# A query scratch laid out by head, its loads moved ahead of the last sums, and maxima turned in another PSUM bank

## The chip, the cores and the metric

One Trainium2 chip, one of its cores. The metric is the device time of one execution in microseconds; of several executions the median counts. The engines are named TensorE (PE in the rows, PEld its weight loads), VectorE (DVE), ScalarE (ACT), GpSimd (POOL) and SyncE (SP); SyncE issues most of the transfers, one after the other.

## What is computed

A block of three sublayers on 4 x 256 tokens of width 512: half a mixture-of-experts step, attention, half a mixture-of-experts step with the same weights. Only the attention matters here:

```python
NUM_HEADS = 32; HEAD_DIM = 16
qkv = hidden_states @ Wqkv
q = qkv[..., :512].reshape(B, S, 32, 16)
k = qkv[..., 512:528]; v = qkv[..., 528:]          # one key and value head for all
scores = einsum('bqhd,bkd->bhqk', q, k) * scale
scores = where(causal, scores + slopes * (pos_k - pos_q), -1e30)
probs = softmax(scores, axis=-1)
attn = einsum('bhqk,bkd->bqhd', probs, v).reshape(B, S, 512)
return attn @ Wo
```

The input is float32, and the scores are formed with float32's accuracy: a query or key value is split into three bfloat16 parts, and a score is the sum of six products of parts.

## The kernel before

The program is written engine by engine. Each engine runs its list in order, and semaphores are the only ties between them. There are four batches (b) of 256 tokens with 32 heads; a group (q, 0 to 7 in a batch) is four heads; n = 8 b + q counts groups over all batches.

**Projections.** In five items per batch (four quarters of the queries, and keys with values) TensorE multiplies, ScalarE takes the first bfloat16 part out of PSUM (L817 for queries, L811 for keys), VectorE forms the rest (L1253), GpSimd the two lower parts (L596, L598). SyncE stores the three parts to DRAM (`q_dram`, L384, and `k_dram`, L382), and loads them back turned, so that the contraction rows of the score products lie on partitions: 96 rows (16 dimensions times six products of parts), for queries in `qside`, for keys in `kT`. ScalarE may write a quarter's first part again only when the store of the batch before has landed.

`qside` has two halves in turn, one for even and one for odd batches, and each batch is loaded in two halves of 16 heads by `q_rows` (L386; its six loads are L394). For batches 2 and 3 this takes place while batches 0 and 1 are attended. Such a load waits for `st_done`, the last use of the rows it overwrites.

**Scores and maxima.** For batch b + 1, `scores` (L1686 to L1688) forms a head's scores with queries on partitions, in two banks in turn, and VectorE reduces each to row maxima (L1264). A product may not start before the maximum of the head two places ahead is taken. Of 16 heads the maxima are joined (L1270), turned by TensorE (`max_turn`, L1721), negated by ScalarE (L839), split by GpSimd (`maxima_parts`, L614 to L617), stored (L407) and loaded as three more rows of `qside` (L410, `m_rows`). In the same groups `scores_t` (L1700, L1702) forms the scores of batch b transposed, with the maxima's rows in the product, ScalarE takes the exponential (L861), GpSimd zeroes the later tokens (L647), and `weigh` (L1714) multiplies by the values into bank `PS_O`. The even groups' results are copied to `aT` (L827), the odd ones' to `odd` (L831). `scores_t` of group 4 needs the second half's maxima of its own batch (`m_in1`).

**Sums.** The values carry columns of ones, so each group's result also holds the sums of the exponentials. SyncE moves them into `sums`: those of an even group by `sums_of_even` (L436), those of an odd one by `odd_in` (L444), which then moves the rest of `odd` into `aT` (L446). When all four pairs of a batch are in, VectorE inverts them in two halves (L1287; L1277 for batch 2), ScalarE and GpSimd split the inverse into parts (L846, L653 to L658), TensorE spreads them over the partitions (`inverse_rows`, L1731), VectorE normalises (L1300), and TensorE multiplies by Wo (`out_part`, L1738). The bank `PS_A` serves `inverse_rows`, `out_part` and, but for the first half of batch 0, `max_turn`. So `max_turn` waits there for the normalisation (q = 4) or for the residual sum (q = 0).

SyncE's order at the end of a batch is: sums of pair 3, odd sums of pair 3, query loads of batch b + 2 (heads 16 to 31), maxima's rows of batch b + 1 (second half). TensorE's order in a group is written out by hand in the loop that begins at L1777.

## Time and profile before

| | us |
|---|---|
| median of 3 runs | 447.17 |
| lowest, highest | 444.88, 447.20 |
| the profiled execution | 446.26 |
| its span, first to last instruction | 444.2 |

Durations in the rows come from the one profiled execution. Times in them are microseconds from the start of its span, so that 2.1 us of its 446.26 lie outside. In the span the first feed-forward stage ends at about 137 us, the projections at about 193 us, the attention at about 313 us; the rest is the second feed-forward stage. The mean granted TensorE clock is 0.985 of full speed.

A timeline row gives the start, the duration, the engine, the line, what is written and read, the number of instructions merged into the row and, in brackets, the idle time of the engine ahead of it with what ended it. A row of SPq is SyncE issuing a transfer, not the transfer. In the chain of waits each piece is the start, the length and what it was.

### The profile page before, as it was taken

The numbers are of one execution on the slowest core, as the hardware profiler recorded it, in microseconds if no ns is written. First come the engines' busy times: TensorE is split into PE (matmuls) and PEld (weight loads), VectorE is DVE, ScalarE is ACT, GpSimd is POOL, SyncE is SP. The second block draws the span as 40 slices with busy tenths as digits, with TensorE's granted clock in tenths as the row PEclk, the third lists the DMA queues.
The fourth block names the chain that finished last, engine by engine and source line by source line (L and its number), as shares of the span: only waits on it lengthen the run. The fifth ranks groups of instructions, "written<-read, shape, count | busy, mean of one in ns | idle before, by whom it ended". The sixth has DMA issues, their size and how long they took to land.

```text
span 444.2 us, 8306 instructions
## 1 busy us (share of the span) xinstructions
PE 394.1 (89%) x2788; PEld 276.5 (62%) x2789; DVE 258.3 (58%) x638; ACT 177.3 (40%) x302; POOL 176.5 (40%) x268
## 2 busy tenths in 40 slices
PE   0799899999969998989979989889999879999972
PEld 0677578888646766555555555344687558888660
DVE  4579643332457975687775685466539933333357
ACT  1321246656202222157654464653340336665300
POOL 2431226666302772355544354452001055666300
PEclk9999999999998999999999999989999999999997
DMA  7999994544289468323133030010420043534278
GB/s 234 291 379 303 316 338 139 176 116 144 111 296 294 131 170 175 96 83 93 29 96 93 8 95 19 10 38 27 155 96 1 0 142 116 161 122 150 90 290 324
DMA packets 51052, 66.05 MB, mean 149 GB/s; under 512 B 8190, under 2 KB 30374, under 8 KB 50980
## 3 DMA queue, kind: packets, MB, share of 16 engines
q1 hardware_dynamic: 42652, 43.55, 31.1%
q0 software_dynamic: 6368, 19.32, 13.9%
q10 hardware_dynamic: 2000, 2.76, 2.0%
q8 instruction: 18, 0.29, 0.3%
q14 instruction: 14, 0.11, 0.1%
HBM read 46.32 MB, written 19.79 MB: 149 GB/s over the span
## 4 chain that ended last, share of the span: by engine, by line
PE 59%; DVE 16%; DMA 12%; SPq 6%; issue 4%; ACT 1%; POOL 1%; ACTq 0%; DVEq 0%; POOLq 0%
PE ps L1588 15%; PE ps L1595 7%; PE ps L1452 6%; PE ps L1738 6%; PE ps L1573 4%; SPq L394 4%; PE ps L1714 3%; PE ps L1657 3%; DMA turns<-in_L_ffn_sw_dram 3%; DMA q_dram<-arena 3%; PE ps L1686 3%; PE ps L1493 2%; DMA arena<-xn_dram,arena 2%; DVE arena L1264 2%; PE ps L1688 2%
## 5 line engine op out<-in xcount | busy, mean ns | idle before, releaser
L1264 DVE TENSOR_REDUCE arena<-ps 128x3 f32<-128x384 f32 x128 | 69.4, 555 | 33.7 <-PE ps L1688 31.6
L1588 PE MATMUL ps<-arena,wj 128*128 128x128 f32 x608 | 74.1, 274 | 0.0
L1588 PEld LDWEIGHTS ps<-arena,wj 128*128 128x128 f32 x608 | 71.0, 192 | 1.0 <-issue 1.0
L861 ACT ACTIVATE arena<-ps 128x768 f32<-128x768 f32 x64 | 51.2, 810 | 43.1 <-PE ps L1702 42.1
L647 POOL TENSOR_SCALAR_AFFINE_SELECT arena<-arena 128x512 f32<-128x512 f32 x64 | 40.7, 641 | 56.7 <-ACT arena L861 56.2
L1159 DVE SCALAR_TENSOR_TENSOR arena<-ps,arena 128x128 f32<-128x128 f32 x38 | 13.3, 351 | 80.1 <-ACT arena L753 80.1
L1452 PE MATMUL ps<-arena,turns 128*128 128x256 f32 x256 | 57.6, 381 | 0.6 <-DMA turns<-in_L_ffn_sw_dram 0.6
L1452 PEld LDWEIGHTS ps<-arena,turns 128*128 128x128 f32 x256 | 48.1, 190 | 9.0 <-issue 2.1
L553 POOL DMA_INDIRECT arena<-xn_dram,arena x34 | 33.2, 978 | 50.8 <-DVE arena L1099 25.2
L558 POOL DMA_INDIRECT y_dram<-arena x38 | 38.4, 1011 | 33.8 <-DVE arena L1166 25.5
L1686 PE MATMUL ps<-cb 128*128 128x256 bf16 x128 | 35.3, 276 | 5.2 <-DVE arena L1264 4.0
L1595 PE MATMUL ps<-w,arena 128*128 x76 | 39.1, 596 | 0.6 <-DVE arena L1159 0.6
L758 ACT COPY wj<-w 128x1024 f32 x38 | 39.6, 1047 | 0.0
L1493 PE MATMUL ps<-turns,arena 128*128 128x512 f32 x64 | 31.9, 623 | 3.6 <-issue 3.6
L749 ACT COPY arena<-ps 128x512 f32<-128x512 f32 x38 | 22.3, 587 | 30.9 <-PE ps L1573 30.9
L1688 PE MATMUL ps<-arena 116*128 116x256 bf16 x128 | 34.6, 270 | 0.0
L1657 PE MATMUL ps<-arena,wj 128*128 128x256 f32 x128 | 31.6, 383 | 1.4 <-ACT arena L801 1.4
L707 ACT ACTIVATE arena<-ps,shb 128x256 f32<-128x256 f32 x16 | 7.6, 473 | 57.9 <-PE ps L1452 57.9
L1738 PE MATMUL ps<-turns,arena 128*128 128x512 f32 x64 | 30.0, 604 | 0.0
L1714 PE MATMUL ps<-arena 128*32 128x128 f32 (+1 forms) x512 | 28.1, 338 | 1.4 <-POOL arena L647 1.4
L1573 PEld LDWEIGHTS ps<-cf,arena 128*128 128x128 f32 x136 | 16.6, 140 | 19.6 <-issue 17.7
L1687 PE MATMUL ps<-arena 116*128 116x128 bf16 x128 | 28.2, 220 | 0.0
(196 smaller groups left out, 586.3 us busy)
## 6 DMA issues: line engine op xcount, KB each, us to landing
arena<-y_dram SPq DMA_DIRECT2D x16, 512.0 KB, 7.4
arena<-q_dram SPq DMA_DIRECT2D x36, 128.0 KB, 2.7
xn_dram<-arena SPq DMA_DIRECT2D x16, 256.0 KB, 5.3
w<-in_L_ffn_ew_dram SPq DMA_DIRECT2D x4, 1024.0 KB, 11.0
q_dram<-arena SPq DMA_DIRECT2D x16, 192.0 KB, 2.4
x<-_attn_hidden_states_dram SPq DMA_DIRECT2D x4, 512.0 KB, 6.2
out_dram<-x SPq DMA_DIRECT2D x8, 256.0 KB, 5.9
arena<-arena SPq DMA_DIRECT2D x30, 64.0 KB
```

What stands on the lines that cost most here:

```text
L647: pool.affine_select(diagonal, diagonal, [[0, 2], [0, 2], [1, P]], ALU.is_ge, 0.0, base=0, channel_multiplier=-1).then_inc(sem("sel"), 1)
L861: act.activation(pr[:, n % 2, pair, :], ps[:, bank:bank + 2, :].rearrange("p a b -> p (a b)")[:, 0:768], ACT.Exp).then_inc(sem("exp"), 1)
L1264: dve.tensor_reduce(m3[:, h // (HEADS // 2), :, h % (HEADS // 2)], ps[:, bank, 0:3 * P].rearrange("p (n k) -> p n k", n=3), AX_X, ALU.max) ...
L1452: ins = pe.matmul(o, sw12[:, c, cols], xnT[:, 2 * pair:2 * pair + 2, c, :], start=(c == 0), stop=(c == KC - 1))
L1493: ins = pe.matmul(ps[:, z_bank(t), :], hidden[t // 2 % 2][:, c, t % 2 * P:(t % 2 + 1) * P], sw3s[:, c, :], start=(c == 0), stop=(c == SHAR ...
L1588: ins = pe.matmul(o, wj[:, par, c, n * INTER:(n + 1) * INTER], xgT[:, par, c, :], start=(c == 0), stop=(c == KC - 1))
L1595: pe.matmul(ps[:, PS_Y + par, :], hj[:, par, :], w3[:, ds(e, 1), :], start=True, stop=True).then_inc(sem(f"y{f}"), 1)
L1657: ins = pe.matmul(ps[:, PS_ST + c, 0:SEQ], wq[:, k, c * P:(c + 1) * P], xaT[b % 2][:, k, :], start=(k == 0), stop=(k == KC - 1))
L1686: pe.matmul(o.rearrange("p (n k) -> p n k", k=P)[:, 0:3:2, :], identb, mask, start=True, stop=True)
L1688: pe.matmul(o[:, P:3 * P], qside[0:R_MAX, p, h, P:2 * P], kT[0:R_MAX, b, :], start=False, stop=True, skip_group_check=True).then_inc(sem(" ...
L1714: ins = pe.matmul(o, vv[:, b, k, 1 - n % 2:1 - n % 2 + 2 * HD], pr_blocks(n % 2, h // 2)[:, k * QT:(k + 1) * QT - k, h % 2, :], start=(k = ...
L1738: ins = pe.matmul(ps[:, at_bank(b, t), :], aT[b % 2][:, c, t * P:(t + 1) * P], wo[:, c, :], start=(c == 0), stop=(c == KC - 1))
```

## The change

It does four things.

- `q_dram` is laid out by batch, head, dimension, part, where it was batch, part, head and dimension. The 96 rows of a product are ordered anew: 48 rows are the three query parts against the first key part, 48 are the query parts 0, 0, 1 against the key parts 1, 2, 1. It is the same six products.
- `q_rows` loads its half with four transfers, one of 48 rows and three of 16, where it had six of 16. The keys are stored by three transfers still, the first of them reading its part three times.
- At the end of a batch, the query loads stand ahead of the odd sums of the last pair.
- `max_turn` writes to the upper half of bank `PS_O`, whose lower half takes the weighed values (but for the first half of batch 0). It is called inside `weigh`, ahead of the weighing, and the next weighing waits until ScalarE has copied the turned maxima. The waits that kept `PS_A` free for it are dropped.

```diff
-QPART = (0, 0, 0, 1, 1, 2)
-KPART = (0, 1, 2, 0, 1, 0)
+QPART = (0, 0, 1)
-        q_dram = nc.dram_tensor("q_dram", (BATCH, 3, DIM, SEQ), BF16).ap()
-        k_dram = nc.dram_tensor("k_dram", (BATCH, HD, len(KPART), SEQ), BF16).ap()
+        q_dram = nc.dram_tensor("q_dram", (BATCH, HEADS, HD, 3, SEQ), BF16).ap()
+        k_dram = nc.dram_tensor("k_dram", (BATCH, 2, HD, 3, SEQ), BF16).ap()
...
-        def m_bank(b, half):
-            return PS_S if (b, half) == (0, 0) else PS_A
+        def turned(b, half):
+            return ps[0:HEADS, PS_S, 0:P] if (b, half) == (0, 0) else ps[0:HEADS, PS_O, SEQ:SEQ + P]
...
-                        for at, count in K_RUNS:
-                            sp.dma_start(k_dram[b, :, at:at + count], kp[:, 0:count]).then_inc(sem("k_out"), 16)
+                        sp.dma_start(k_dram[b, 0], kp[:, 0:1].to_broadcast([HD, 3, SEQ])).then_inc(sem("k_out"), 16)
+                        sp.dma_start(k_dram[b, 1, :, 0:2], kp[:, 1:3]).then_inc(sem("k_out"), 16)
+                        sp.dma_start(k_dram[b, 1, :, 2], kp[:, 1]).then_inc(sem("k_out"), 16)
                     else:
-                        sp.dma_start(q_dram[b, :, c * P:(c + 1) * P, :].rearrange("k p t -> p k t"), qp[:, :, c, :]).then_inc(sem(f"q_out{c}"), 16)
+                        sp.dma_start(q_dram[b, c * 8:(c + 1) * 8].rearrange("h d k t -> (h d) k t"), qp[:, :, c, :]).then_inc(sem(f"q_out{c}"), 16)
...
-                for r in range(len(QPART)):
-                    sp.dma_start(qside[r:R_REST:SPREAD, p, first:last],
-                                 q_dram[b, QPART[r], first * HD:last * HD].rearrange("(h d) t -> d h t", d=HD)
+                sp.dma_start(qside[0:3 * HD, p, first:last], q_dram[b, first:last].rearrange("h d k t -> (d k) h t")
+                             ).then_inc(sem(f"q_in{p}{0 if first == 0 else 1}"), 16)
+                for r in range(3):
+                    sp.dma_start(qside[3 * HD + r:R_REST:3, p, first:last],
+                                 q_dram[b, first:last, :, QPART[r]].rearrange("h d t -> d h t")
                                  ).then_inc(sem(f"q_in{p}{0 if first == 0 else 1}"), 16)
...
                 sums_of_even(4 * b + 3)
-                odd_in(4 * b + 3)
                 if b + 2 < BATCH:
                     q_rows(b + 2, HEADS // 2, HEADS)
+                odd_in(4 * b + 3)
...
+            behind = [0]
+
-            def weigh(n):
+            def weigh(n, turn=None):
 
                 b = n // 8
-                pe.wait_ge(sem("sel"), 2 * n + 2)
                 if n >= 1:
                     pe.wait_ge(sem("oT"), n)
+                if turn is not None:
+                    pe.wait_ge(sem("m_copy"), 2 * turn[0] + turn[1])
+                    max_turn(*turn)
+                    behind[0] = 2 * turn[0] + turn[1] + 1
+                elif behind[0]:
+                    pe.wait_ge(sem("m_copy"), behind[0])
+                    behind[0] = 0
+                pe.wait_ge(sem("sel"), 2 * n + 2)
...
             def inverse_rows(b, half):
 
                 pe.wait_ge(sem("inverse"), b + 1)
-                pe.wait_ge(sem("m_copy"), min(2 * b + 4 + half, 2 * BATCH))
-                if half == 1:
+                if b >= 1:
+                    pe.wait_ge(sem("att_x"), QT * b)
+                if half == 1 and inverse_bank(b, 1) == PS_A:
                     pe.wait_ge(sem("normed"), 2 * b + 1)
...
                     if n >= 1:
-                        weigh(n - 1)
-                    if q == 0:
-                        if b >= 2:
-                            pe.wait_ge(sem("att_x"), QT * (b - 1))
-                        max_turn(b, 1)
-                    if q == 4 and more:
-                        if b == 0:
-                            pe.wait_ge(sem("m_copy"), 2)
-                        else:
-                            pe.wait_ge(sem("normed"), 2 * b - 1)
-                        max_turn(b + 1, 0)
+                        weigh(n - 1, (b, 1) if q == 0 else (b + 1, 0) if q == 4 and more else None)
+                    elif n == 0:
+                        pe.wait_ge(sem("m_copy"), 1)
+                        max_turn(0, 1)
+                        behind[0] = 2
```

SyncE's list at the end of batch 0 (the same at the end of batch 1), before: the even and odd sums of pair 3, the six query loads (L394), the store and the two loads of the maxima's rows.

```order
L436 DMA arena<-arena 4x256 [waits oT]
L444 DMA arena<-arena 4x256 [waits oT]
L446 DMA arena<-arena 64x256 [waits even_sums1]
L394 DMA arena<-q_dram 16x16x256 [waits st_done,q_out3,q_out2]
L394 DMA arena<-q_dram 16x16x256 x5
L407 DMA m_dram<-arena 32x3x128 [waits m_parts]
L410 DMA arena<-m_dram 3x16x128 [waits m_out]
```

The same place in the changed kernel, whose lines lie four further on (L440, L448 and L450 are the sums, L395 and L398 the query loads, L411 and L414 the maxima's rows):

```order
L440 DMA arena<-arena 4x256 [waits oT]
L395 DMA arena<-q_dram 48x16x256 [waits st_done,q_out3,q_out2]
L398 DMA arena<-q_dram 16x16x256 x3
L448 DMA arena<-arena 4x256 [waits oT]
L450 DMA arena<-arena 64x256 [waits even_sums1]
L411 DMA m_dram<-arena 32x3x128 [waits m_parts]
L414 DMA arena<-m_dram 3x16x128 [waits m_out]
```

Four query loads now stand between the even and the odd sums, and the maxima's store follows the odd sums directly.

TensorE's list at the end of the fifth group (q = 4) of batch 1, before: the weighing (L1714), the turned maxima (L1721), scores of the next group, and further down the second half of the spread inverse (L1731).

```order
L1714 MATMUL ps<-arena 32x256 [waits oT,sel]
L1714 MATMUL ps<-arena 32x256 x3
L1714 MATMUL ps<-arena 32x128 x4
L1721 MATMUL ps<-cf,arena 32x128 [waits m_nm,normed]
L1686 MATMUL ps<-cb 128x2x128 [waits s_max]
...
L1731 MATMUL ps<-arena,cb 128x256 [waits normed,m_copy,inverse]
```

The same place in the changed kernel (L1734 turns the maxima, L1727 weighs, L1745 spreads the inverse):

```order
L1734 MATMUL ps<-cf,arena 32x128 [waits m_nm,m_copy,oT]
L1727 MATMUL ps<-arena 32x256 [waits sel]
L1727 MATMUL ps<-arena 32x256 x3
L1727 MATMUL ps<-arena 32x128 x4
L1690 MATMUL ps<-cb 128x2x128 [waits s_max]
...
L1745 MATMUL ps<-arena,cb 128x256 [waits normed,inverse]
```

The turned maxima moved ahead of the weighing, and the wait for the normalisation went from them.

## Rows read from the trace of the kernel before

**Rows 1.** The page's part 1: busy us (share of span) and instructions of each engine.
```profile
PE 394.1 (89%) x2788; PEld 276.5 (62%) x2789; DVE 258.3 (58%) x638; ACT 177.3 (40%) x302; POOL 176.5 (40%) x268
```

**Rows 2.** Timeline of SyncE in the projections: start, us, line, transfer.
```profile
149.27 1.25 SPq L382 DMA_DIRECT2D k_dram<-arena  x3
...
158.93 3.82 SPq L394 DMA_DIRECT2D arena<-q_dram  x6
162.79 3.81 SPq L382 DMA_DIRECT2D k_dram<-arena  x3
```

**Rows 3.** The chain of waits in the projections: start, us, what.
```profile
167.12 2.31 DMA q_dram<-arena
...
174.20 6.05 DMA q_dram<-arena
```

**Rows 4.** Timelines of ScalarE and TensorE in the projections, idle time in brackets.
```profile
168.78 0.37 ACT L811 ACTIVATE arena<-ps 16x256 bf16<-16x256 f32 x1 [4.45 <-DMA k_dram<-arena]
...
180.33 0.88 ACT L817 CAST arena<-ps 128x256 bf16<-128x256 f32 x2 [4.45 <-DMA q_dram<-arena]
...
170.45 0.28 PE L1686 MATMUL ps<-cb 128*128 128x256 bf16 x1 [0.96 <-DVE arena L1264]
...
181.76 0.28 PE L1686 MATMUL ps<-cb 128*128 128x256 bf16 x1 [0.98 <-DVE arena L1264]
```

**Rows 5.** Windows: stretch, engines' busy us, TensorE clock, DMA share, GB/s.
```profile
166.00:167.00 1.00, 1.00 (x7) 0.46 (x6) 0.44 (x1) 0.00 (x0) 0.34 (x1) 1.00 0.59 129
...
175.00:176.00 1.00, 0.25 (x3) 0.07 (x1) 0.86 (x3) 0.58 (x1) 0.46 (x2) 1.00 1.21 185
```

**Rows 6.** Timeline of SyncE at the end of batch 0.
```profile
220.16 0.50 SPq L446 DMA_DIRECT2D arena<-arena  x1
220.77 5.06 SPq L394 DMA_DIRECT2D arena<-q_dram  x6
225.88 0.61 SPq L407 DMA_DIRECT2D m_dram<-arena  x1
```

**Rows 7.** Timeline of TensorE, end of batch 0 and fifth group of batch 1.
```profile
217.82 0.27 PE L1702 MATMUL ps<-arena 119*128 119x256 bf16 x1
...
228.35 0.27 PE L1688 MATMUL ps<-arena 116*128 116x256 bf16 x1
230.48 0.38 PE L1700 MATMUL ps<-arena 119*128 119x512 bf16 x1 [1.85 <-DMA arena<-m_dram]
...
234.03 0.28 PE L1721 MATMUL ps<-cf,arena 128*32 128x128 f32 x1 [0.46 <-DVE arena L1300]
```

**Rows 8.** Timelines of VectorE and SyncE where reciprocals start, batches 0 and 2.
```profile
222.09 0.95 DVE L1287 RECIPROCAL arena<-arena 128x128 f32<-128x128 f32 x1
...
224.69 3.36 DVE L1264 TENSOR_REDUCE arena<-ps 128x3 f32<-128x384 f32 x6
...
285.87 0.50 SPq L446 DMA_DIRECT2D arena<-arena  x1
...
287.77 1.75 DVE L1277 RECIPROCAL arena<-arena 128x256 f32<-128x256 f32 x1 [2.71 <-DMA arena<-arena]
```

**Rows 9.** Timelines of GpSimd and TensorE, the inverse of batch 0.
```profile
228.74 0.66 POOL L658 TENSOR_TENSOR arena<-arena 128x256 bf16<-128x256 f32 x1
...
231.08 0.82 PE L1731 MATMUL ps<-arena,cb 128*128 128x256 bf16 x6
```

**Rows 10.** Timelines of GpSimd and TensorE, the same place of batch 2.
```profile
262.56 0.66 POOL L658 TENSOR_TENSOR arena<-arena 128x256 bf16<-128x256 f32 x1
...
263.37 0.38 PE L1700 MATMUL ps<-arena 119*128 119x512 bf16 x1 [0.89 <-DMA arena<-m_dram]
...
263.98 0.82 PE L1731 MATMUL ps<-arena,cb 128*128 128x256 bf16 x6
```

**Rows 11.** The loads of L394: issue ns min/median/max, first and last start.
```profile
L394 SPq DMA_DIRECT2D arena<-q_dram x42: 560/609/1769, 151.1 to 258.0; - x42
```

**Rows 12.** Window in batch 3, columns as in rows 5.
```profile
292.00:294.00 2.00, 2.00 (x13) 0.84 (x15) 1.15 (x2) 0.69 (x1) 0.00 (x0) 0.50 0.10 33
```

## What the change will do: the prediction

> **What bounds the kernel now.** I read the page's busy shares first, then the chain that ended last through the attention stage (140 to 312 us), then the idle time of TensorE in that stage with its releasers, and last SyncE's issue times, because all edits but one sit on that queue. TensorE is busy 89% of the span [rows 1]; the two feed-forward stages touch nothing of the change, so its price is the sum of the waits of TensorE that it shortens or makes. Three places count.
>
> *The projections, 155 to 181 us.* The chain runs over SyncE: a block of six query loads takes 3.82 us to issue, three key stores behind it 3.81 us (elsewhere the same three took 1.25), then a query store lands, then the next block of loads, then a store issued at 174.20 that lands 6.05 us later [rows 2, 3]. ScalarE waits 4.45 us for the key stores and again 4.45 us for that store; TensorE loses only 0.96 and 0.98 us to the two, 1.94 in all [rows 4]. While the second block drains, the DMA engines are full and move 185 GB/s [rows 5].
>
> *The fifth group of batch 1, 228 to 231 us.* TensorE stands 1.85 us for the maxima's rows [rows 7]. They are late since their store is issued at 225.88, behind six query loads (5.06 us) that are themselves behind the odd sums' two copies, the second issued at 220.16 [rows 6]. The same group of batch 2 stands 0.89 us [rows 10].
>
> *The normalisation's wait.* At 234.03 TensorE waits 0.46 us for VectorE before it turns the maxima, as both use one PSUM bank [rows 7]. This stands twice, in batches 1 and 2.
>
> **The change, part by part.**
>
> *Four loads for six.* Same bytes, same 512 B pieces. One load takes 0.609 us (median of 42, 0.56 at least) [rows 11], with the gap behind it 0.65; each block of six becomes 2.6 us for 3.9, so 1.3 us less. The new first load has three times the rows of the others. No row shows a load of that form; the 256 KB loads among the 42 have twice the rows of the 128 KB ones, and the median and minimum hold for both, so I take 0.65 for it too. In the projections the block at 158.93 ends 1.3 us earlier, so key stores, the store at 167.12, the next block and the landing at 180.25 follow 1.3 earlier, if nothing else holds them. Bounds: 0, if the 3.81 us of the key stores is the queue waiting for the loads to drain (then they end when they did); 1.94, all that TensorE loses there, if those stores also fall towards their 1.25. The second block's faster issue gives nothing: its 1.5 MB drain at the DMA engines' rate and the store lands behind them. I take **-1.3**.
>
> *The layout.* Query stores become 384 rows of 512 B in place of 128 times three, the first key store 48 rows in place of 16. They are as many bytes over the same queue; I take 0, with the two bounds just given as its bounds too.
>
> *The loads ahead of the last odd sums.* SyncE may start when the last transposed scores of batch 0 are done, 217.82 + 0.27 = 218.1 [rows 7]. Four loads end at 220.7; the two copies follow at 220.7 and 221.3, and the maxima's store at 221.85 in place of 225.88. Its rows land about 4 us earlier, TensorE needs them only 2.0 us earlier (the product began at 230.48; the one ahead of it at 228.35, so it stood ready at about 228.45), so that wait goes.
>
> But a wait takes its place. The second copy is issued at 221.3 in place of 220.16, 1.1 us later. VectorE's reciprocal started at 222.09, 1.93 us after that copy's issue; at 285.87 and 287.77, with nothing in the queue and VectorE plainly waiting, the distance is 1.90 [rows 6, 8]. So the reciprocal hangs on this copy already, without slack, and behind it VectorE is booked to 228, its last six maxima without a gap [rows 8]. Call its delay D. It is 1.1 at least. With 786 kB of loads ahead in the queue the copy lands no sooner than 218.1 + 1.9 + their transfer: at 185 GB/s (4.25 us) 224.25, D = 2.2; at 202 GB/s, which the loads reach with no backlog (131 kB in 0.65 us), 3.9 us and D = 1.8. Below 3.2 us of transfer D is 1.1. The short block lies nearer to the free-running case, which issue alone limits, so I take 1.5.
>
> In the projections' trace the store issued behind 1.5 MB of loads took 6.05 us, so small transfers do wait their turn [rows 3]. The Trainium skill (DMA: Bandwidth & Descriptors, Queues, rings and completion order) says the same: on each DMA engine the descriptors of one issuing queue are consumed in ring order. By that rule alone the moved loads would always cost the sums their whole transfer; by the latency alone they cost the 1.1 us of issue.
>
> VectorE's delay passes whole to TensorE, whose scores wait for each maximum. So the wait of 2.03 us gives 2.03 - D. Then another wait stands up: the low part of the inverse, from GpSimd, was ready at 228.74 + 0.66 = 229.40, hangs on the same reciprocal and moves by D too; the product that spreads it stood at 231.08 and can now start at 229.5 + D [rows 9]. Gain there 1.58 - D. For batch 2 the product stood at 263.98 and the inverse was ready at 263.22 [rows 10]: 0.66 - D, that is, a loss.
>
> *Turning the maxima in the other bank.* It removes the two 0.46 us waits. TensorE goes on to scores whose maxima are done; the next consumer, the second half of the spreading, wants that same normalisation, which ended just before 234.03, and TensorE gets there a group's half later, about 234.5. So 0.46 each, nothing late behind. The new order puts one transposition ahead of the weighing and makes the next weighing wait for ScalarE's copy; that copy comes directly behind ScalarE's output copy, a whole group ahead of the next weighing, so 0. In batch 3, where the sums' path sets the end, the transposition counts once: its row lists 0.28 us, of which pipelining hides the most, so +0.1 [rows 7]. The dropped waits for the last maxima copy were long met: 0.
>
> **Sum.** Batch 1: 1.58 + 0.46 - D = 2.04 - 1.5 = 0.54 gained. Batch 2: 0.66 + 0.46 - 1.5 = 0.38 lost. Projections 1.3 gained, batch 3 0.1 lost: -1.3 - 0.54 + 0.38 + 0.1 = **-1.4 us**. Against the profiled execution that is 442.8 us of span, 444.9 of 446.3 in time; that execution lies 0.9 us below the median, so on the median 447.2 - 1.4 = **445.8 us**.
>
> **Rivals.**
>
> *All of it comes:* the key stores fall back, D = 1.1. -1.94 - 0.94 - 0.02 + 0.1 = -2.8, 444.4 us. For: three stores at 1.25 us show that 3.81 is not their own cost. Against: it needs both, and the stall at 163 may stand elsewhere again (a load at 222 took 1.77 us with no visible reason, the maximum in rows 11).
>
> *The issue time is no bound:* nothing in the projections, D about 1.8. -0.24 + 0.68 + 0.1 = +0.5, 447.7 us. For: the longest piece of that chain, 6.05 us, is a landing behind a full queue [rows 3]. Against: SyncE issues without a gap from 158.93 to 166.65.
>
> *The sums drown behind the loads (slower).* Place: the last odd copy of batches 0 and 1. If four larger loads are fed faster than the engines take them, at 302 GB/s against 202 before, and they drain as slowly as the row at 166 us (129 GB/s with the engines only 0.59 busy) [rows 5], say 142, the transfer is 5.5 us and D = 3.5: 1.46 + 2.38 + 0.1 - 1.3 = +2.6, 449.8 us. Moved loads lose as soon as D passes 2.2 in both batches, even with the projections' gain; by over 0.5% from 3.3. Against: 185 GB/s is the rate at the deepest queue the trace has.
>
> *The clock.* At 292 to 294 us TensorE ran 2.00 us at a granted 0.50, 1.2 GHz, behind waits of over 1 us [rows 12]. Those waits stay, but if the fall comes at another moment, what ran in this row takes half: 1.0 us less, 444.8; or as much more, should one fall come at the new waits.
>
> **How the numbers follow.** A measurement of this kernel tells about 0.5% (2.2 us) from no change. Forecast 0.42, all of it 0.26, no bound at issue 0.14, drowned sums 0.12, clock helping on top of the forecast (443 to 445) 0.06. Faster by over 0.5%: 0.26 + 0.06 = 0.32; slower: 0.12; within: 0.56. The forecast's own range runs from D = 1.1 (445.0) to no gain in the projections and D = 2.2 (-(-0.16) + 1.08 + 0.1 = +1.3, 448.5). The range reaches down to the full gain with the clock's 1.0 (443.3) and up to 448.8, short of the drowned case.
>
> **What would show it.** Blocks of loads at 2.6 us; key stores of batch 1 under 2.5 us or still 3.8; ScalarE's second 4.45 us wait about as long, but ended near 179. TensorE's 1.85 and 0.89 us waits for the maxima's rows gone, VectorE's first reciprocal 1.1 to 2.2 us behind its last maximum, released by a transfer, and short TensorE waits for maxima and for the inverse behind it. No wait on the normalisation ahead of the turned maxima. I am wrong if the reciprocal's delay is over 2.2, if the wait for the maxima's rows stays, or if the first large load takes well over 0.65 us to issue.

## The result and the profile after

The changed kernel takes **449.27 us** (median of 17 executions, 446.54 to 455.52), the kernel before, run beside it on the same chip, 446.03 (17, 443.41 to 449.73). The ratio is 1.0075, 95% interval 1.0048 to 1.0103: some 3 us slower. The forecast was 445.8 with a range up to 448.8, so it was wrong, and in sign. Ratios here and below leave disturbed executions out, the medians do not, so that the two can differ (most where the loads alone were moved, six of ten left out).

The profiled execution has a span of 448.7 us against 444.2. I cut both at three events on TensorE: the first projection product, the first main score, and the transposition of the fourth token tile in the second feed-forward, which waits for VectorE in both:

| stretch | before | after | difference |
|---|---|---|---|
| up to the projections | 137.83 | 136.39 | -1.44 |
| projections | 55.71 | 60.01 | **+4.30** |
| main attention | 118.83 | 118.02 | -0.81 |
| second feed-forward | 131.83 | 134.28 | +2.45 |

The first and last rows hold no edit. In the twelve whole kernels of this study the last row lies between 131.7 and 135.1 us with the same code in it, so its 2.45 is nothing that the change can be blamed for on one execution. The projections are where the change lost; the forecast had -1.3 there.

The projections as one window, before and after (columns as in [rows 5]: the first is the length, the next TensorE's busy time, the last three clock, DMA share and GB/s):

```profile
137.83:193.54 55.71, 50.84 (x291) 36.73 (x289) 41.24 (x91) 13.52 (x33) 28.36 (x50) 1.00 0.61 147
...
136.39:196.40 60.01, 52.48 (x290) 37.18 (x289) 41.24 (x91) 13.41 (x33) 28.38 (x50) 0.97 0.65 133
```

Of the 4.30 us, 2.66 are idle time of TensorE (7.53 against 4.87) and 1.64 are the same products taking longer at a lower clock. Over the whole span TensorE's busy time grew by 5.8 us (399.9 against 394.1).

SyncE's timeline in the projections (start, us, line, transfer), beside [rows 2]. L395 is the 48-row load, L398 the three 16-row loads, L382 to L384 the key stores, L328 the load of the turned keys, L386 query stores:

```profile
157.93 0.32 SPq L395 DMA_DIRECT2D arena<-q_dram  x1
158.30 1.94 SPq L398 DMA_DIRECT2D arena<-q_dram  x3
160.28 0.61 SPq L382 DMA_DIRECT2D k_dram<-arena  x1
160.93 0.58 SPq L383 DMA_DIRECT2D k_dram<-arena  x1
161.56 0.83 SPq L384 DMA_DIRECT2D k_dram<-arena  x1
162.43 3.26 SPq L386 DMA_DIRECT2D q_dram<-arena  x2
...
168.54 0.32 SPq L395 DMA_DIRECT2D arena<-q_dram  x1
168.91 4.37 SPq L398 DMA_DIRECT2D arena<-q_dram  x3
173.32 2.54 SPq L328 DMA_DIRECT2D arena<-k_dram  x1
175.91 1.36 SPq L386 DMA_DIRECT2D q_dram<-arena  x2
```

Up to 162 us all went as forecast or better: the block issues in 2.3 us, not 3.82, and the key stores in 2.1, not 3.81. Nobody got anything from it: SyncE's stall moved to the two query stores behind, 3.26 us where the same two took 0.95 before (at 166.65). The waits of ScalarE and TensorE for what the stores carry, idle time in brackets, beside [rows 4]:

```profile
168.05 0.37 ACT L815 ACTIVATE arena<-ps 16x256 bf16<-16x256 f32 x1 [5.11 <-DMA k_dram<-arena]
...
181.61 0.85 ACT L821 CAST arena<-ps 128x256 bf16<-128x256 f32 x2 [6.44 <-DMA q_dram<-arena]
...
169.72 0.28 PE L1690 MATMUL ps<-cb 128*128 128x256 bf16 x1 [1.62 <-DVE arena L1268]
...
183.03 0.28 PE L1690 MATMUL ps<-cb 128*128 128x256 bf16 x1 [2.97 <-DVE arena L1268]
```

The two TensorE waits grew by 0.66 and 1.99 us, together 2.65 of these 2.66. The key stores were issued earlier, 1.1 us by the stretch's own time, and landed 0.7 later. The query store of the second wait was itself issued 3.1 us later in the stretch (at 175.91, 174.20 before [rows 3]): SyncE had been held up, 4.37 us at three loads and 2.54 at the one behind them (3.91 for six and 0.68 before). The reason shows in a window of the second block's drain; the two behind it show what TensorE then lost on top:

```profile
173.00:175.00 2.00, 1.47 (x13) 1.05 (x11) 1.42 (x4) 0.79 (x2) 0.26 (x1) 1.00 1.19 106
184.00:186.00 2.00, 2.00 (x8) 0.68 (x7) 0.87 (x3) 0.27 (x1) 1.06 (x2) 0.57 0.01 4
230.00:232.00 2.00, 2.00 (x21) 0.80 (x19) 0.92 (x2) 0.81 (x1) 0.64 (x1) 0.50 0.07 23
```

With the DMA engines as full as in [rows 5] (1.19 against 1.21) they move 106 GB/s, not 185; two us earlier it is 151, and from 176 us on 204 again. And behind its 2.97 us wait TensorE's granted clock fell to 0.57, near the lower of its levels, 1.2 GHz; it was 0.58 in the two microseconds after.

The other place of the forecast, the last odd sums: SyncE at the end of batch 0 (beside [rows 6]), then VectorE's reciprocal and TensorE (beside [rows 8] and [rows 7]):

```profile
220.31 0.38 SPq L395 DMA_DIRECT2D arena<-q_dram  x1
220.73 1.94 SPq L398 DMA_DIRECT2D arena<-q_dram  x3
...
223.33 0.53 SPq L450 DMA_DIRECT2D arena<-arena  x1
224.44 0.31 SPq L411 DMA_DIRECT2D m_dram<-arena  x1
```

```profile
227.27 0.95 DVE L1291 RECIPROCAL arena<-arena 128x128 f32<-128x128 f32 x1 [2.45 <-DMA arena<-arena]
...
228.69 0.40 PE L1690 MATMUL ps<-cb 128*128 128x256 bf16 x1 [2.69 <-DVE arena L1268]
...
262.14 0.28 PE L1690 MATMUL ps<-cb 128*128 128x256 bf16 x1 [0.56 <-DVE arena L1268]
```

The copy of L450 is issued at 223.33 and the reciprocal that it releases starts at 227.27, 3.9 us later, where that takes 1.90 with an empty queue [rows 8]. So the reciprocal stood 2.45 us, TensorE 2.69, and then ran at 0.50 of its clock for two microseconds. The 1.85 and 0.89 us waits for the maxima's rows and the two of 0.46 are gone, as forecast. In batch 2 the wait that came in their place is 0.56 only, where 0.34 stood before: SyncE had issued the loads from 252.20 on, and the odd copy that follows them in its program came at 258.18, held by ScalarE and not by them.

```profile
252.20 0.38 SPq L395 DMA_DIRECT2D arena<-q_dram  x1
...
258.18 0.57 SPq L448 DMA_DIRECT2D arena<-arena  x1
```

### The profile page after: what moved, and what is told of

The parts are those of the page before. It is cut to its first block, busy times and chain, and to the rows that moved or that the text cites. A ratio compares the mean times of both kernels' runs of the same rounds, so it can differ in the third digit from the quotient of the medians.

```text
span 448.7 us, 8286 instructions
## 1 busy us (share of the span) xinstructions
PE 399.9 (89%) x2788; PEld 280.1 (62%) x2789; DVE 258.3 (58%) x638; ACT 176.8 (39%) x302; POOL 176.4 (39%) x268
## 4 chain that ended last, share of the span: by engine, by line
PE 59%; DVE 17%; DMA 11%; issue 4%; POOL 3%; ACT 2%; SPq 2%; ACTq 1%; DVEq 0%; POOLq 0%
PE ps L1592 15%; PE ps L1599 7%; PE ps L1752 6%; PE ps L1456 5%; PE ps L1577 4%; PE ps L1661 4%; PE ps L1727 3%; PE ps L1690 3%; DMA arena<-xn_dram,arena 2%; DMA arena<-arena 2%; DVE arena L1268 2%; PE ps L1692 2%; DMA x<-_attn_hidden_states_dram 2%; PE ps L1704 2%; DMA k_dram<-arena 1%
## 5 line engine op out<-in xcount | busy, mean ns | idle before, releaser
L1592 PE MATMUL ps<-arena,wj 128*128 128x128 f32 x608 | 75.8, 278 | 0.0
L1592 PEld LDWEIGHTS ps<-arena,wj 128*128 128x128 f32 x608 | 72.7, 195 | 1.0 <-issue 1.0
L1497 PE MATMUL ps<-turns,arena 128*128 128x512 f32 x64 | 33.3, 646 | 3.5 <-issue 3.5
L1690 PEld LDWEIGHTS ps<-cb 128*128 128x128 bf16 x128 | 12.4, 97 | 31.4 <-DVE arena L1268 22.0
L1752 PE MATMUL ps<-turns,arena 128*128 128x512 f32 x64 | 30.0, 604 | 0.0
L1727 PE MATMUL ps<-arena 128*32 128x128 f32 (+1 forms) x512 | 28.1, 338 | 1.6 <-POOL arena L651 1.6
```

The lines of the kernel that those rows point to most:

```text
L1592: ins = pe.matmul(o, wj[:, par, c, n * INTER:(n + 1) * INTER], xgT[:, par, c, :], start=(c == 0), stop=(c == KC - 1))
L1690: pe.matmul(o.rearrange("p (n k) -> p n k", k=P)[:, 0:3:2, :], identb, mask, start=True, stop=True)
L1727: ins = pe.matmul(o, vv[:, b, k, 1 - n % 2:1 - n % 2 + 2 * HD], pr_blocks(n % 2, h // 2)[:, k * QT:(k + 1) * QT - k, h % 2, :], start=(k = ...
L1752: ins = pe.matmul(ps[:, at_bank(b, t), :], aT[b % 2][:, c, t * P:(t + 1) * P], wo[:, c, :], start=(c == 0), stop=(c == KC - 1))
```

## The experiments

Two questions stood at once: does the loss come from the place of the loads or from their form, and if from the form, from which part of it. In what follows "near" is the changed kernel's order of rows (the 48-row load on partitions 0 to 47, the 16-row ones on every third of 48 to 95), "spread" is the 48-row load on every second of 0 to 95 and the others on every sixth. The stretches named are those of the table.

**The place of the loads, taken back.**

```diff
-                if b + 2 < BATCH:
-                    q_rows(b + 2, HEADS // 2, HEADS)
                 odd_in(4 * b + 3)
+                if b + 2 < BATCH:
+                    q_rows(b + 2, HEADS // 2, HEADS)
```

> The changed kernel with one part undone: the query loads of heads 16 to 31 stand behind the last odd sums again. Theory A (the sums drown behind loads that drain at about 130 GB/s in this form, where the old form drained at 185 or was limited by issue): VectorE's first reciprocal of batch 0 starts 1.9 us after the copy's issue again, not 3.8; TensorE's 2.7 us wait for a maximum goes; the wait for the maxima's rows comes back, about 1 to 2 us; the projections keep their loss of about 2.5 us, since their second block of loads is the same. Time 1 to 2 us under the changed kernel, 1 to 2 us over the kernel before. Theory B (the move alone made the loss): the time falls to that of the kernel before or under it, and the projections show no loss.

448.2 us median, ratio 1.0050 (1.0009 to 1.0092). VectorE's wait for the copy fell from 2.45 to 0.26 us, and the wait for the maxima's rows came back with 1.59 and 1.44 us. It is still slower than the kernel before, with its projections at 57.87 us. Its 2.16 us over the kernel before there are nearly all clock: TensorE is busy for 52.70 us against 50.84 and idle for 5.17 against 4.87, while in the changed kernel 2.66 us were idle time. The change of 0.25 points in the ratio (0.01 is one point) lies within the intervals, so that this run alone prices neither the place nor the rest; it shows that the place is not all of the loss.

**Six loads again, in the new layout and near.**

```diff
...
-                sp.dma_start(qside[0:3 * HD, p, first:last], q_dram[b, first:last].rearrange("h d k t -> (d k) h t")
-                             ).then_inc(sem(f"q_in{p}{0 if first == 0 else 1}"), 16)
+                for k in range(3):
+                    sp.dma_start(qside[k:3 * HD:3, p, first:last], q_dram[b, first:last, :, k].rearrange("h d t -> d h t")
+                                 ).then_inc(sem(f"q_in{p}{0 if first == 0 else 1}"), 16)
```

> The changed kernel with its 48-row load cut into three 16-row loads; DRAM layout, order of rows, place of the loads all as changed. If the form of the 48-row load is slow (its 48 rows lie on 48 neighbouring partitions): blocks of loads flow at 185 to 200 GB/s again, land in 2.5 to 2.8 us each where alone, the store behind the second block of the projections lands about 2.5 us earlier than in the changed kernel, and the time falls by 2 to 4 us. If the DRAM layout is slow (heads 24 KB apart, dimensions 1.5 KB apart, where it was 8 KB and 512 B): loads still land in 4.5 us at 130 to 150 GB/s and the time stays within 1 us of the changed kernel. If the rows' order in SBUF is the cause (16-row loads on every third of 48 neighbouring partitions, where it was every sixth of 96), it would look the same as the layout; the run with spread rows tells those two apart.

452.06 us, ratio 1.0138 (1.0089 to 1.0188), the slowest of all; projections 61.79 us, waits for the stores 5.88 and 6.65 (the profiled execution is the slowest of its five). So the single 48-row load is not needed for the loss. What is left is the layout in DRAM or the order of rows.

**The changed kernel with its rows spread.** Four loads as in the change, the keys' rows permuted in the same way (not shown):

```diff
...
-                sp.dma_start(qside[0:3 * HD, p, first:last], q_dram[b, first:last].rearrange("h d k t -> (d k) h t")
+                sp.dma_start(qside[0:R_REST:2, p, first:last], q_dram[b, first:last].rearrange("h d k t -> (d k) h t")
...
-                    sp.dma_start(qside[3 * HD + r:R_REST:3, p, first:last],
+                    sp.dma_start(qside[2 * r + 1:R_REST:6, p, first:last],
```

> The changed kernel with its rows ordered so that the 48-row load goes to every second of 96 partitions and the three 16-row loads to every sixth; four loads and the DRAM layout of queries as changed (the keys' rows follow). If 48 neighbouring partitions are the cause: the 384 KB load lands in about 3.5 us where it took 4.6, the DMA engines move 185 GB/s or more in the blocks, and the time falls by 2 to 4 us. If the DRAM layout or the size of the load is the cause: 4.5 us and 130 to 150 GB/s as in the changed kernel, the time within 1 us of it.

446.42 us, ratio 1.0041 (1.0001 to 1.0080); projections 56.13 us. In the drain's window (172 to 174 us here) the engines move 205 GB/s at the same share:

```profile
172.00:174.00 2.00, 1.25 (x7) 0.87 (x6) 0.85 (x3) 0.58 (x1) 1.06 (x2) 1.00 1.19 205
```

The large load of batch 1's block in the window 160 to 190 us (median us from issue to landing, last), first of the changed kernel, then of this one:

```profile
arena<-q_dram SPq DMA_DIRECT2D x1, 768.0 KB, 8.8
```

```profile
arena<-q_dram SPq DMA_DIRECT2D x1, 768.0 KB, 6.3
```

**Six loads, spread**, which is the kernel before's form but for the layout in DRAM (the same permuted rows, the 48-row load cut in three).

> The changed kernel with its DRAM layout (by head, dimension, part), but with six loads per half, each onto every sixth of 96 partitions, which is the row order of the kernel before. If neighbouring partitions are what halves the rate and the DRAM layout is harmless: the projections' stretch is as long as before's (first main score 55 to 56.5 us after the first projection matmul, ScalarE's wait for the second query load about 4.5 us), and what is lost is the longer issue ahead of the last odd sums alone: reciprocal waits 3.5 to 4 us, time 1 to 2.5 us over before. If the DRAM layout slows the reads: the projections' stretch is 58 us or more, as with six loads onto neighbouring rows, ScalarE's wait 6 us, and the time 5 us or more over before.

448.24 us, ratio 1.0047 (1.0012 to 1.0082). Projections 56.39 us, second wait 4.49: the layout in DRAM costs nothing. VectorE waited 3.48 us in batch 1, for a block that issues in 3.85 us, not 2.6.

**Spread, and the loads behind the sums:** both suspected losses taken out.

> The changed kernel with rows spread and the second half's loads back behind the last odd sums: what is left of the change is four loads instead of six, the new layout and the maxima's turn. If near rows and the place ahead of the sums are the two losses, both are gone: reciprocal in batch 1 waits under 0.5 us, the maxima wait ahead of scores is 0.5 to 1.8 us (1.5 to 1.9 before) since fewer issues stand ahead of the maxima's store, projections' stretch 55 to 57 us, time 0.5 to 2 us under before. If something else in the change costs: 1 us or more over before. If four loads are worth nothing against six: as the kernel with the turn alone, within 0.5 us of before.

444.44 us, ratio 0.9946 (0.9908 to 0.9984). By the expectation's last case four loads are then not worth nothing: this kernel against the one with the turned maxima alone (0.9995, below) is four loads against six behind the sums, 0.49 points faster with some 0.4 of uncertainty. TensorE's waits for the maxima's rows are 1.26 and 0.65 us here, 1.54 and 0.84 there.

So four pairs of kernels differ in the rows. The difference is in points of the ratio, with the uncertainty that the two intervals give together; "released" is when the landed query store ends ScalarE's second wait, counted from the first projection product:

| pair | near | spread | difference | projections, us | TensorE idle in them | released |
|---|---|---|---|---|---|---|
| four loads, ahead of the sums | 1.0075 | 1.0041 | 0.34 ± 0.48 | 60.01, 56.13 | 7.53, 5.28 | 45.2, 42.9 |
| six loads, ahead | 1.0138 | 1.0047 | 0.91 ± 0.61 | 61.79, 56.39 | 8.40, 5.55 | 46.2, 43.2 |
| four loads, behind | 1.0050 | 0.9946 | 1.04 ± 0.56 | 57.87, 56.09 | 5.17, 5.25 | 44.7, 42.9 |
| as the first, odd batches alone spread | 1.0075 | 1.0022 | 0.53 ± 0.43 | 60.01, 57.23 | 7.53, 6.33 | 45.2, 44.0 |

Near rows are the slower in all four; in the first pair, which is the changed kernel itself, the difference in time is within its uncertainty. The last column is the steadiest: 44.7 to 46.2 us in the three near kernels, 44.0 in the mixed one and 42.5 to 43.2 in all eight others. In the third pair the near kernel shows no idle time more. Its clock fell behind its first wait (1.49 us) to 0.56 and 0.59 for 170 to 174 us, so that TensorE took 1.86 us longer over the work ahead and ScalarE came late to its second wait and stood 4.22 us, not 6.44: what the late store costs there stands in the busy time.

The four kernels with four loads also price the place: ahead of the sums costs 0.95 ± 0.55 points spread and 0.25 ± 0.50 near, close rows 0.34 and 1.04. Counted so, place and rows weigh about the same, 0.6 and 0.7 points on average, each with some 0.4 of uncertainty.

The last pair is a run that asked which batch it is:

```diff
...
-                sp.dma_start(qside[0:3 * HD, p, first:last], q_dram[b, first:last].rearrange("h d k t -> (d k) h t")
+                sp.dma_start(qside[0:R_REST:2, p, first:last] if p else qside[0:3 * HD, p, first:last], q_dram[b, first:last].rearrange("h d k t -> (d k) h t")
```

> The changed kernel with spread rows for batches 1 and 3 alone; batches 0 and 2 have near rows, loads ahead of the last odd sums as in the change. If the loss of the projections' stretch is the batch 1 block of 1.5 MB on near rows, ahead of stores that ScalarE waits for: ScalarE's wait for the second query store falls from 6.44 us to about 4.5, the stretch from 60.0 us to 56 or 57, and the kernel is 2 to 3 us under the changed one (0 to 1 us over before). If it is batch 0's half blocks: the stretch stays over 58.5 us and the time within 1 us of the changed kernel's. Loads and the sums' wait in batch 1 of the attention are batch 2's, near, so the reciprocal still waits about 2.4 us.

446.24 us, ratio 1.0022 (0.9989 to 1.0054). ScalarE's wait for the second query store is 4.57 us, TensorE's behind it 1.10. So the block of 1.5 MB that fills batch 1's queries, all heads at once, is one part of what the stores stood behind. Batch 0's two half blocks, still near, are another of about the same size: TensorE's idle time fell by 1.20 us, ScalarE's release came 1.2 us earlier, and both stay 1.1 us short of the kernel with all rows spread (ScalarE's wait for the key stores is 5.78 us).

**The loads by themselves.** A program that does nothing else: SyncE issues one form, waits until it has landed, issues the next.

> No attention and no feed-forward: the output is the input copied. It measures the loads by themselves: SyncE issues a half's loads (768 KB of 512 byte pieces) in one form, waits until all have landed, and goes to the next form, three times over: six loads from the old layout and six from the new one onto every sixth of 96 rows (spread), six onto every third row of 48 (near), four of the changed kernel (near), four spread, a 48-row load alone in both row orders, a 16-row load alone on rows at steps of 6, 3 and 1, the 64 KB copy of the odd sums alone, and the copy behind four loads. If rows close together halve the rate whoever else runs: four near take 1.5 us or more longer than four spread, six near as much over six spread, and a 48-row load near moves 384 KB at 115 to 150 GB/s against 185 or more spread. If the slow rate in the kernel came from the stores and computing beside the loads: near and spread within 0.3 us of each other here. If the layout in DRAM matters: six spread from the new layout differ from six of the old by over 0.5 us. The copy behind four loads lands 2 to 4 us later than alone after near loads, 0.5 to 2 later after spread ones, by the first theory.

SyncE's timeline of the first round; a form takes from its first start to the next form's:

```profile
23.58 3.94 SPq L69 DMA_DIRECT2D six_old<-by_part  x6
29.64 1.86 SPq L72 DMA_DIRECT2D six_spread<-by_head  x3
...
35.59 1.86 SPq L77 DMA_DIRECT2D six_near<-by_head  x3
...
41.90 0.56 SPq L81 DMA_DIRECT2D four_spread<-by_head  x1
...
47.61 0.34 SPq L85 DMA_DIRECT2D four_near<-by_head  x1
...
53.75 0.55 SPq L89 DMA_DIRECT2D one_spread<-by_head  x1
57.53 0.32 SPq L91 DMA_DIRECT2D one_near<-by_head  x1
61.88 0.55 SPq L93 DMA_DIRECT2D one_step<-by_head  x1
...
70.12 0.55 SPq L99 DMA_DIRECT2D even<-odd  x1
71.96 0.56 SPq L101 DMA_DIRECT2D four_spread<-by_head  x1
...
78.03 0.31 SPq L106 DMA_DIRECT2D four_near<-by_head  x1
```

Six old 6.06 us, six spread from the new layout 5.95, six near 6.31, **four spread 5.71**, four near 6.14; a single 48-row load 3.78 spread, 4.35 near. Over the three rounds six old take 5.74 to 6.06 us, six spread 5.80 to 6.05, six near 6.31 to 6.59, four spread 5.71 to 5.97 and four near 6.01 to 6.51. Two things follow. Half a batch costs 0.3 to 0.6 us more near: real, but far from the 1.5 that I had expected, and no explanation yet for 4 us. And four loads land hardly sooner than six, though they are issued in 2.5 us instead of 3.9: the drain is the bound. The odd sums' copy takes 1.84 us alone (70.12 to 71.96). Behind four spread loads it takes 6.07 from the block's start, of which 2.6 is issue, so that it lands 3.5 us after its own issue (3.9 and 3.7 in the other rounds); behind four near ones 4.0 and 4.3.

**A store behind the loads**, with and without VectorE and ScalarE working:

> Again no attention and no feed-forward, the output is the input copied. SyncE issues a half's loads in one of four forms (six or four, rows spread or near), then two 192 KB stores of query parts, and waits until the stores have landed; four times over, the last two while VectorE and ScalarE copy tiles without pause. If a store queued behind near loads lands later because it stands behind transfers that take longer: block and stores take 0.4 to 1 us longer near than spread, with and without the engines' work. If near loads hurt only while the engines use SBUF: no difference over 0.3 us in the first two turns, 1 us or more in the last two. If neither: under 0.3 us everywhere, and what near rows cost in the kernel stays open.

Block and two stores, from this run's timeline: four spread 6.32, 6.21, 6.37 and 6.45 us, four near 7.10, 6.95 and 6.54; six spread 7.10 to 7.26, six near 7.20 to 7.31. The engines' work makes near rows no dearer, and they cost 0.2 to 0.8 us with four loads and 0.2 at most with six. Still too little.

**The whole batch's block**, 1.5 MB as for batch 1:

> No attention and no feed-forward, the output is the input copied. As the run with the stores behind half a batch's loads, but with the block that the projections' stretch has for batch 1: all 32 heads, 1.5 MB, in the same four forms, with two stores of 192 KB behind it, three times over, other engines idle. If near rows cost what they do by the number of bytes in one block (two bounds from the kernels: the 768 KB load of that block lands after 8.0 and 8.8 us near, 6.3 and 6.7 us spread): block and stores take 1.5 to 3 us longer near than spread, twice to four times the 0.2 to 0.8 us of half a batch. If the cost is by half a batch as measured and only doubles: 0.4 to 1.5 us. If it is none of the loads' own: under 0.4 us, and the rest is the kernel's other transfers.

The timeline's first round:

```profile
43.39 0.57 SPq L78 DMA_DIRECT2D fourspread<-by_head  x1
44.00 2.82 SPq L80 DMA_DIRECT2D fourspread<-by_head  x3
...
53.79 0.32 SPq L85 DMA_DIRECT2D fournear<-by_head  x1
54.16 3.30 SPq L87 DMA_DIRECT2D fournear<-by_head  x3
57.50 1.83 SPq L88 DMA_DIRECT2D aside<-source  x1
59.38 1.02 SPq L89 DMA_DIRECT2D aside<-source  x1
66.22 1.91 SPq L63 DMA_DIRECT2D sixspread<-by_head  x3
```

Four spread with the stores 10.40, 10.35 and 10.30 us; four near 12.43 (53.79 to 66.22) and 12.30. Six loads do the same: 10.44 to 10.93 spread, 12.23 to 12.73 near. The 768 KB load lands in 6.1 us spread and 7.9 near (medians), in the kernels in 6.3 and 8.8. Near costs 2.0 us per whole batch, and SyncE itself is held up, 3.30 us where 2.82 was, then 1.83 and 1.02 for two stores; the kernel's timeline has the like in its 4.37 and 2.54 us. The cost grows faster than the bytes; that a half block's drain lies mostly beside its issue and its latency would explain it, but no run shows that. In the kernels ScalarE's release came 1.8 to 3.0 us later with all rows near (the table's first three pairs), about this much. That 6.44 against 4.45 us of ScalarE's second wait is 1.99 as well is in part chance, as the 4.22 us of the third pair's near kernel show.

**Which rows take longer.** Single loads of all heads that differ in one thing at a time:

> No attention and no feed-forward, the output is the input copied. Single loads of all 32 heads from the new layout, each waited for: 48 rows (768 KB) onto partitions 0 to 47, 40 to 87, 64 to 111, and every second of 0 to 95; then 16 rows (256 KB) onto every fourth of 0 to 63, every fourth of 32 to 95, onto 0 to 15, 56 to 71, every second of 0 to 31, and every sixth of 0 to 95. If it is closeness of rows that costs: 48 close rows take the same wherever they lie, about 7.2 us (2 of latency and 5.2 at the 150 GB/s of the single near load measured before), spread ones 5.8. If it is that all rows lie on one side of partition 64: 0 to 47 and 64 to 111 take about 7.2, but 40 to 87 only 5 to 6 us although its rows are as close; of the 16-row loads every fourth of 32 to 95 is faster than every fourth of 0 to 63, and 56 to 71 than 0 to 15. The Trainium skill (SBUF - State Buffer, Door 1: The DMA port swizzle) states the second: partitions 0 to 63 reach only half of the ports, and which half depends on the side of 64.

```profile
20.77 0.32 SPq L57 DMA_DIRECT2D low<-by_head  x1
28.06 0.31 SPq L59 DMA_DIRECT2D across<-by_head  x1
33.66 0.30 SPq L61 DMA_DIRECT2D high<-by_head  x1
41.26 0.67 SPq L63 DMA_DIRECT2D spread<-by_head  x1
47.11 0.55 SPq L65 DMA_DIRECT2D low<-by_head  x1
```

| 48 rows, 768 KB | three rounds, us | 16 rows, 256 KB | three rounds, us |
|---|---|---|---|
| 0 to 47 | 7.29, 7.66, 7.69 | every fourth of 0 to 63 | 3.41, 3.48, 3.32 |
| 40 to 87 | **5.60, 5.77, 5.45** | every fourth of 32 to 95 | 3.13, 3.14, 3.06 |
| 64 to 111 | 7.60, 7.50, 7.22 | 0 to 15 | 4.59, 4.26, 4.83 |
| every second of 0 to 95 | 5.85, 6.15, 6.18 | 56 to 71 | 4.69, 4.52, 4.54 |

Two more forms: 16 rows on every second of 0 to 31 take 3.37 to 3.54 us, on every sixth of 0 to 95 3.15 and 3.42. Rows 40 to 87 are as close together as 0 to 47 and 2 us faster: closeness alone is not it, the side of partition 64 matters. One expectation of that theory fell: 16 rows across 64 are no faster than 0 to 15. So the side is not all of the rule.

The Trainium skill (SBUF — State Buffer, Door 1: The DMA port swizzle) has a rule that covers the eight of the table: a transfer is limited by how many of 16 ports its partitions reach; four partitions in a row share one, 32 further on is the same one again, 64 further on another. By it the 48-row loads reach 8, 12, 8 and 16 ports, the 16-row ones 8, 16, 4 and 4. This run agrees, with about 7.5 us for 8 ports, 5.6 and 6.1 for 12 and 16, and, in the order of the table, 3.4, 3.1, 4.6 and 4.6 for the 16-row loads; only that 12 were no slower than 16 doesn't follow from the count. Worked out further from the page, the fullest port holds 8, 4, 8 and 4 rows, and 2, 1, 4 and 4: an estimate that puts the loads of each size in their order, and no more than that.

**The maxima's bank alone**, on the kernel before: their transposition goes to the weighed values' bank.

> The kernel before with one part of the change alone: maxima turned in the weighed values' bank, ahead of the weighing. By the prediction's step TensorE's two waits of 0.46 us on the normalisation go and nothing comes in their place: 0.8 to 0.9 us faster than the kernel before (445.2 where that has 446.0). Rival: the waits reappear at the next product that wants the normalisation (0 us), or the copies' place makes the weighing wait (slower, by up to 0.5 us).

444.69 us, ratio 0.9995 (0.9972 to 1.0018). The two 0.46 us waits are gone; a gain of 0.9 us lies inside this interval, and so does none.

**The move alone**, on the kernel before:

> The kernel before with one part of the change: the six query loads of the second half stand ahead of the last odd sums' copy; layout, row order and bank of the maxima as before. If a block of loads ahead of the copy is what the sums wait for, whatever its form: the block takes 3.8 to 5.1 us of issue, so VectorE's reciprocal in batch 1 waits about 3.5 to 4 us for the copy (0.2 with the loads behind it), the maxima wait of 1.5 to 1.9 us goes, and the kernel is 1.5 to 3 us slower than before. If only the changed kernel's form of loads made the sums late: the reciprocal waits under 1 us and the time is within 1 us of before or 1 to 2 us under it.

449.5 us median of ten (442.19 to 453.64), ratio 0.9996 (0.9945 to 1.0046): the time is inconclusive. The trace is not. VectorE waits 3.08 us for the copy, TensorE 3.32 where 0.38 was; the two kernels with six loads of the new layout ahead of the sums show the same wait of VectorE, 3.48 us spread and 3.78 near. The clearest measure of the move is the spread pair, ahead 1.0041, behind 0.9946: 0.95 points, some 4 us with 2.5 of uncertainty, where the profiled attention stages differ by 2.10 us (near: 0.25 points, within the intervals, and 1.25 us).

**The store first.** If loads cost what is queued behind them, the small and urgent transfer should go ahead. On the kernel before with the new bank, the maxima's store goes first, then the loads, then the rows' loads, which must wait for that store anyway:

```diff
                 sp.dma_start(m_dram[p, :, half].rearrange("k r q -> r k q"), mp[:]).then_inc(sem("m_out"), 16)
+                if between is not None:
+                    between()
                 sp.wait_ge(sem("m_out"), 16 * (2 * b + half + 1))
...
-                if b + 2 < BATCH:
-                    q_rows(b + 2, HEADS // 2, HEADS)
                 if b + 1 < BATCH:
-                    m_rows(b + 1, 1)
+                    m_rows(b + 1, 1, (lambda: q_rows(b + 2, HEADS // 2, HEADS)) if b + 2 < BATCH else None)
```

> The kernel before with the maxima turned in the weighed values' bank, and on SyncE the store of the maxima first, then the six query loads of the second half, then the maxima's two loads; all behind the last odd sums. If the maxima's wait ahead of scores comes from their store standing behind six issues (5.1 us) and its landing being waited for by SyncE: the store's landing lies beside the issues, the waits of 1.5 to 1.9 us (batch 1) and 0.8 us (batch 2) fall under 0.5 each with no wait of the sums, and the time is 1.5 to 2.5 us under before. If the store or the maxima's loads are slowed as much by the query transfers beside them: the waits stay within 0.5 us of what they were, and the time is within 0.5 us of before.

**442.84 us**, ratio 0.9934 (0.9898 to 0.9969), faster than both kernels. SyncE, and TensorE where 1.85 us stood:

```profile
220.42 0.31 SPq L407 DMA_DIRECT2D m_dram<-arena  x1
220.85 5.22 SPq L394 DMA_DIRECT2D arena<-q_dram  x6
226.12 0.81 SPq L412 DMA_DIRECT2D arena<-m_dram  x2
```

```profile
228.33 0.27 PE L1686 MATMUL ps<-cb 128*128 128x256 bf16 x1 [1.14 <-DMA arena<-q_dram]
229.14 0.38 PE L1700 MATMUL ps<-arena 119*128 119x512 bf16 x1 [0.37 <-DMA arena<-m_dram]
```

My expectation of under 0.5 us in batch 1 was wrong: 1.51 us of 1.85 are left, now mostly put down to the query loads. Batch 2's 0.89 is gone, and the sums wait 0.25 us as ever. With the two 0.46 us waits that is 2.2 us from the trace, for 2.9 in the ratio.

**The same with four loads, spread:**

> The changed kernel with spread rows (48-row load onto every second of 96 partitions, the 16-row ones onto every sixth) and the second half's query loads behind the last odd sums and between the maxima's store and their loads. By the theory that neighbouring partitions and the block ahead of the sums are the two losses, nothing of them is left, and the fewer issues (2.4 us a block instead of 5.1) count: reciprocal waits under 0.5 us, no maxima wait over 0.5 us, projections' stretch 53 to 55.5 us, time 2 to 3.5 us under before. If the fewer issues are worth nothing: as the store-first kernel in the same call, within 0.5 us. If another part of the change costs something (maxima turn held behind weighing): within 1 us of before.

443.74 us, ratio 0.9951 (0.9915 to 0.9986): as the one before it within the intervals, and the projections, 55.95 us, are above the 53 to 55.5 that fewer issues were to give. With the maxima's store ahead of the block, four loads have nothing on six that can be measured.

## Why the prediction was wrong, step by step

**"The layout. [...] As many bytes over the same queue; I take 0."** This is the step that failed. Bytes, pieces and queue were the same, but the rows in SBUF were not: the reordering that makes one load of three puts all 48 of its rows on one side of partition 64, where each load had spanned both. It costs 2.0 us per 1.5 MB, shown in the loads' own run, and the kernel has that block ahead of a store that ScalarE, VectorE and TensorE wait for in turn. In place of -1.3 the projections gave +4.30: 2.66 us of idle time, which the late stores explain, and 1.64 us of lower clock, which no term of the sum had and whose tie to the rows is not shown. I had priced the DRAM side, which indeed costs nothing (six old 5.74 to 6.06 us, six spread 5.80 to 6.05), and never the SBUF side, though the diff shows the rows' steps as plainly as the pieces. The bounds given, 0 and 1.94 of gain, excluded a loss without a reason.

**"Four loads for six: -1.3."** Wrong as well in the projections, apart from the rows. The kernels with four spread loads issue the block 1.1 to 1.3 us faster and have projections of 55.95 to 56.13 us; those with six old loads have 55.71, 56.04, 56.33 and 57.42 (1.7 of the last is lower clock). By themselves four spread take 5.71 to 5.97 us, six old 5.74 to 6.06. The key stores did fall from 3.81 to 2.1 us, towards the 1.25 of the upper bound, and nothing came of it, since the stall went to the query stores behind them (3.26 us), as the first rival's "against" had feared, and all of them land behind the drain. The rival "the issue time is no bound" had the projections right. In the attention stage, where the maxima's store stands behind the block, fewer issues do seem to be worth something: the 0.49 points above.

**The loads ahead of the sums.** The structure held: the maxima's waits gone, the reciprocal late, released by a transfer, TensorE late by as much. The size did not: D was taken as 1.5 us; the wait was 2.45 near, 2.19 spread and 3.48 for six spread. The 185 GB/s bound would have said 2.2, and I had chosen the smaller for being a short block. The copy behind it has to wait for the drain all the same: it lands 1.84 us after its issue alone, and 3.5 to 3.9 behind four spread loads. "Over 2.2" was also the one sign of being wrong on my list that came; none of the three stood for a loss in the projections. Batch 2 was foreseen as a loss of 0.38 and was a gain: its loads were out of the way before the sums' copies, which there waited for ScalarE, so that the reciprocal stood only 0.32 us. The part was forecast as 0.76 us of loss (1.58 and 0.66, less 1.5 each); ahead against behind, the profiled attention stages differ by 2.10 us spread and 1.25 near, so it was priced too low. Over all the main attention changed by -0.81 us for the -0.06 forecast, so that what overthrew the forecast lies in the projections.

**The slower rival** named the right sign and the wrong place. Its drain of 142 GB/s was near the mark (106 and 151 GB/s in two windows), but it was put at the short block, where D came to 2.45 and not 3.5, instead of at the long one in the projections.

**The clock.** The mean granted clock over the 17 executions was 0.978, against 0.984 for the kernel before in 25. Over the executions of one kernel, 0.01 of that mean goes with 3.5 us in the changed one and 3.7 in the kernel before, so 0.006 would be an estimated 2 us of the 3, in line with the 1.64 us of the projections; waits and clock move together there, so that this is no cause apart from them. In the stretch 130 to 200 us it was 0.95 in all three near kernels and 1.00 in all with spread rows, but 0.95 to 0.98 in those with the old loads too. That is a correlation, not a cause shown: the kernel with the turned maxima alone, with old loads, fell to 0.63 and 0.51 behind a wait of 1.75 us (180 to 184 us), and the odd-spread kernel had TensorE waits of 2.30 and 2.94 us with the clock at 1.00 behind both. What decides whether it falls stays open. Open as well is how the pairs match: in the order of the table the near kernels lost 0.34, 0.91 and 1.04 points (1.5, 4.1 and 4.6 us) on their spread partners, while the profiled projections differ by 3.9, 5.4 and 1.8 us; the first of these is within its uncertainty, and how much of the whole 0.75% is rows, place and clock is not settled more finely than the experiments say.

## What to carry to other kernels

Cost a reordered load on both sides: which partitions its rows land on belongs to its price as much as its bytes, and fewer issues give nothing where the drain is the bound, as in these projections. A queue's large transfers delay what stands behind them by their drain, and not only by their issue, so the small urgent transfer belongs ahead of them: with the maxima's store there and the new bank the kernel is 0.66% faster than before; with the loads ahead of the sums the spread kernel is 0.95 points slower than with them behind. And give an edit taken at zero a bound on the losing side, unless a reason excludes one.

## What the runs showed of the hardware

A 48-row load of 768 KB takes 7.2 to 7.7 us onto partitions 0 to 47 or 64 to 111 and 5.5 to 5.8 onto 40 to 87; 256 KB take 3.1 us on 16 rows of every fourth of 32 to 95 and 4.3 to 4.8 on 16 rows in a block. What a load takes to issue says nothing of this: 0.30 to 0.32 us for adjacent rows, whichever way they land, and 0.53 to 0.67 for stepped ones. The share of time in which the DMA engines are busy does not tell how well they do: 1.19 stood beside 106 GB/s and beside 205 GB/s (the spread kernel, 172 to 174 us). The layout in DRAM (512 byte pieces 1.5 KB apart, or 512 bytes) made no difference to reads, 5.80 to 6.05 and 5.74 to 6.06 us.
